# Second attention of a graph kernel: sums in the step of their scores, and three DVE operands kept in PSUM

## The reference, cut to what matters

```
xp = (x @ W).reshape(n, H, C)                        # H = 4 heads, C = 64
a_src = einsum('nhc,hc->nh', xp, att_src)
a_dst = einsum('nhc,hc->nh', xp, att_dst)
alpha = leaky_relu(a_src[src] + a_dst[dst], 0.2)
amax = segment_max(alpha, dst)
ex = exp(alpha - amax[dst])
denom = segment_sum(ex, dst)
agg = segment_sum(xp[src] * (ex / denom[dst])[..., None], dst)
out = elu(agg.reshape(n, H * C) + bias)
x = layernorm(x + out)
```

## Time and profile before

| what | value |
|---|---|
| median of 3 runs | 5005.02 us (5001.28 to 5005.71) |
| profiled execution, its own time | 5004.25 us |
| its span in the trace | 5002.2 us |
| mean granted TensorE clock | 0.739 of full speed |
| PE busy | 3443.0 us (69%) |
| POOL busy | 3316.7 us (66%) |
| DVE busy | 3196.3 us (64%) |

### The profile page before, as it was taken

How to read it: one execution, slowest core, us unless ns; L and a number is a source line. 1 busy time by engine, 2 the same in 40 slices (tenths; PEclk the granted TensorE clock), 3 DMA queues, 4 the chain that set the end, 5 groups by cost and what they waited for, 6 DMA issues and landing times.

```text
span 5002.2 us, 159594 instructions
## 1 busy us (share of the span) xinstructions
PE 3443.0 (69%) x54244; PEld 2420.8 (48%) x54244; DVE 3196.3 (64%) x9015; ACT 1477.6 (30%) x3981; POOL 3316.7 (66%) x3229
## 2 busy tenths in 40 slices
PE   7978988888888888888455455555545455555554
PEld 4645555555555555555344343444434343444433
DVE  3236888888888888888645555555555555555555
ACT  2325555555555555555200101101000100101011
POOL 1227777777777777777267767777776777676763
PEclk9989999999999999999755555555555555555555
DMA  6879999899999999998234444444444444444443
GB/s 211 282 219 266 266 271 266 265 266 264 266 266 266 266 264 266 267 266 266 83 103 125 120 119 120 117 123 116 122 122 119 118 121 121 118 122 116 124 115 82
DMA packets 690509, 924.71 MB, mean 185 GB/s; under 512 B 351175, under 2 KB 526880, under 8 KB 690208
## 3 DMA queue, kind: packets, MB, share of 16 engines
q0 software_dynamic: 200064, 627.60, 42.6%
q1 hardware_dynamic: 488830, 291.63, 21.8%
q10 hardware_dynamic: 1314, 0.99, 0.1%
HBM read 791.40 MB, written 127.61 MB: 184 GB/s over the span
## 4 chain that ended last, share of the span: by engine, by line
PE 25%; POOL 9%; DMA 9%; issue 5%; DVE 2%; POOLq 0%; ACT 0%; DVEq 0%; SPq 0%
POOL plain_rows L1386 9%; DMA plain_rows<-xp,plain_index 9%; PE plain_p_o L1512 8%; PE plain_p_o L1515 4%; PE plain_p_a L1477 4%; PE plain_p_a L1478 3%; PE plain_p_s L1491 2%; PE plain_p_o L1520 1%; PE plain_p_o L1524 1%; DVE plain_damped L1553 1%; DVE plain_score L1555 1%; PE plain_p_a L1480 1%; PE plain_p_a L1481 1%; PE plain_p_s L1492 0%; PE plain_p_a L1483 0%
## 5 line engine op out<-in xcount | busy, mean ns | idle before, releaser
L1386 POOL DMA_INDIRECT plain_rows<-xp,plain_index x1563 | 1748.5, 1119 | 807.6 <-issue 436.9
L840 POOL DMA_INDIRECT typed_rows<-kv,typed_index x1563 | 1495.8, 957 | 564.1 <-issue 442.2
L1477 PE MATMUL plain_p_a<-plain_a_dst,plain_home 128*128 128x16 f32 x786 | 230.1, 373 | 1089.0 <-DMA plain_rows<-xp,plain_index 1062.5
L1477 PEld LDWEIGHTS plain_p_a<-plain_a_dst,plain_home 128*128 128x128 f32 x786 | 208.9, 326 | 1099.5 <-issue 1099.4
L949 PE MATMUL typed_p_s<-typed_kt,typed_q 64*32 64x416 f32 x4168 | 471.8, 520 | 202.4 <-issue 160.4
L1241 ACT ACTIVATE typed_weight<-typed_weight,typed_col 128x416 f32<-128x416 f32 x521 | 334.8, 643 | 878.1 <-DVE typed_col L1073 849.9
L1044 DVE TENSOR_TENSOR typed_kt<-typed_p_kt,typed_rel 128x768 f32<-128x768 f32 x521 | 494.1, 948 | 5.2 <-PE typed_p_kt L926 5.1
L1071 DVE CUSTOM_DVE_ANT_0 typed_weight<-typed_p_s,typed_far 128x416 f32<-128x416 f32 x521 | 305.6, 587 | 296.6 <-PE typed_p_s L949 270.0
L1512 PE MATMUL plain_p_o<-plain_rows,plain_spread 128*32 128x65 f32 x12504 | 461.1, 315 | 3.8 <-DVE plain_spread L1594 3.8
L926 PE MATMUL typed_p_kt<-all_cst,typed_rows 128*128 128x128 f32 x3126 | 429.0, 274 | 11.2 <-DMA typed_rows<-kv,typed_index 10.5
L1553 DVE TENSOR_SCALAR plain_damped<-plain_p_a 128x64 f32<-128x64 f32 x131 | 29.5, 225 | 596.0 <-PE plain_p_a L1483 596.0
(11 more groups left out here) (224 smaller groups left out, 6610.5 us busy)
## 6 DMA issues: line engine op xcount, KB each, us to landing
typed_match<-match SPq DMA_DIRECT2D x131, 208.0 KB
agg<-qkv_zero SPq DMA_DIRECT2D x98, 264.0 KB, 2.5
typed_agg<-agg SPq DMA_DIRECT2D x98, 264.0 KB
plain_agg<-agg SPq DMA_DIRECT2D x98, 264.0 KB, 3.8
kv<-qkv_kv SPq DMA_DIRECT2D x98, 258.0 KB
typed_kinds<-match SPq DMA_DIRECT2D x131, 192.0 KB
typed_rows<-kv,typed_index POOLq DMA_INDIRECT x1563
plain_rows<-xp,plain_index POOLq DMA_INDIRECT x1563
```

Source lines behind the costliest of these rows:

```text
L840: pool.indirect_dma_start(rows[:, r, j, :], None, k.kv, bass.IndirectOffsetOnAxis(ap=index[:, g, at:at + 1], axis=0)).then_inc(rows_in[r], 16)
L1386: pool.indirect_dma_start(rows[:, r, i, j, :], None, k.xp, bass.IndirectOffsetOnAxis(ap=index[:, g, at:at + 1], axis=0)).then_inc(rest_in[ ...
L1477: pe.matmul(p_a[:, at:at + LANES], home[:, j * P:j * P + P], a_dst[:, m], start=True, stop=False, skip_group_check=True)
```

## The change

PE's list has `aggregate` behind `turn_tops`, with a lag of 1 in place of 2: in a step PE makes the scores of batch b, turns them, turns its maxima, and makes its sums. The lags of all other parts stay. Three operands of DVE move from SBUF into a PSUM tensor `p_x` that was used at the start of the stage only: `running` (written and read by the scans, bank 0), `weight` (written by ACT, read by L1594) and the row of node numbers, copied there once (read by L1578; both in bank 1).

```diff
-        running = z.sb("running", [P, SLOTS])
-        weight = z.sb("weight", [P, KEYS])
+        running, weight, line = p_x[:, 0, 0:SLOTS], p_x[:, 1, 0:KEYS], p_x[:, 1, KEYS:KEYS + TN]
...
-            by_batch(pe, PE_FIRST, PE_UNROLL, BatchPart(1, add_scores), BatchPart(1, turn_scores), BatchPart(2, aggregate), BatchPart(1, turn_tops))
+            by_batch(pe, PE_FIRST, PE_UNROLL, BatchPart(1, add_scores), BatchPart(1, turn_scores), BatchPart(1, turn_tops), BatchPart(1, aggregate))
...
                 v.tensor_tensor(one[:].rearrange("p (e i) n -> p e i n", i=TPB),
-                                cst[:, C_LINE:C_LINE + TN].unsqueeze(1).unsqueeze(1).broadcast_to((P, EDGES, TPB, TN)),
+                                line.unsqueeze(1).unsqueeze(1).broadcast_to((P, EDGES, TPB, TN)),
...
-                                weight[:].rearrange("p (e h) -> p e h", h=HEADS).unsqueeze(3).broadcast_to((P, EDGES * TPB, HEADS, TN)),
+                                weight.rearrange("p (e h) -> p e h", h=HEADS).unsqueeze(3).broadcast_to((P, EDGES * TPB, HEADS, TN)),
...
+            then(v.tensor_copy(line, cst[:, C_LINE:C_LINE + TN]))
             v.sem_inc(setup, 1)
...
-                act.activation(weight[:], gap[:], ACT.Exp).then_inc(exp_done, 1)
+                act.activation(weight, gap[:], ACT.Exp).then_inc(exp_done, 1)
```

## The result

The changed kernel takes 4854.79 us (median of 4 runs, 4849.29 to 4858.85) against 5005.36 before: a ratio of 0.970 (95% interval 0.9683 to 0.9717), 3.0% faster. The forecast was 4770 us. The result lies inside the stated range, at its very end, with 151 us gained in place of 235.

The account below looks back on a forecast made before the run. PE and POOL wait for each other in a ring. The new ring, 2231 us, after 2492.46 and before a 33.6 us tail makes 4757; 10 for late join and 2.05 around it lead to 4770 us, range 4735 to 4860.

Parts of the forecast that it names:

- The ring: New chain from scores through scans, spread and sums to next scores: 16.15 us a step, 17.36 with a block of nodes.
- The tail behind the last sums: Stores, loads and last blocks after the stage's last sums: 33.6 us, in both versions.
- the hand-over: From the end of the sums to the next scores on PE: 0 us, upper bound 0.2.
- the 8 us that it removed: PE's idle time each old step for three gathers and their landing, about 8 us, gone with the new order.
- join late: Slow a_dst DMAs sometimes delay join and the scans, by up to 1.8 us; 10 us added over 95 steps.
- PSUM costs nothing: DVE operations reading PSUM operands take no longer: 0 us taken, loss bound 0.5 us a step or 65 us.
- PSUM gains nothing in this order: POOL has slack in the new ring, so its calls freed by PSUM operands are worth 0.
- the old ring: Before the change: sums, three gathers with landing, scores, turn, sums; steps of 19.1 us with PE and POOL waiting for each other.
- (a): Rival: loads late in most block steps, a ring of 18.6 us of its own, 4875 us; chance 0.07.
- (c): Rival: broadcasting from PSUM at half rate slows L1594 and L1578, 2.66 us a step, 5118 us; chance 0.04.
- (b): Rival: PSUM operands don't free POOL, calls stay stretched, 17.8 us a batch, 4860 us; chance 0.07.
- (d): Rival: PE's granted clock rises from 5 tenths, 3 us a step go, 4390 us; chance 0.04.

Follow-up runs that it names:

- the run with the blocks moved: Changed kernel with PE's loop of 42 steps, join and weigh_parts moved behind spread_weights on DVE, scale behind weigh on ACT: 4655.96 us, ratio 0.9305.
- the last run: Kernel before with three operands in PSUM and 4 slots of rows, plus join moved between find_tops and mark_nodes on DVE: 4541.64 us, ratio 0.9087.

## Why the prediction came out as it did

- **The ring: right.** Sum 16.15 and 17.36 us, measured 16.15 and 17.48. Most of the 0.12 is in leak to first scan (2.47 for my 2.40) and in the sums (5.42 for 5.36). The tail behind the last sums was 33.6 us, and is 33.2.
- **The step that failed is the hand-over:** "The next scores follow at once, their rows, home and a_dst being there; I take 0 for the hand-over, and 0.2 as the upper bound." In 20 of 130 steps it is about 4.2 us, the turn of PE's loop: 20 x 4.16 = 83 us, nearly all of what was missed (4854.79 less 4770 is 85). The run with 42 steps a turn, 4777.97 us, lands 8 from the forecast. That it is so near is in part luck: block steps that are 0.12 us longer add 11 us, and the 10 us for a late join did not come. The turn was in the kernel before too, at the same place, and the profile of before could not show its price: it put PE's idle time down to the rows, which came later still. That is what the prediction should have asked of the 8 us that it removed: what else ends within them.
- **join late: wrong by its 10 us.** In 3000 to 4700 DVE waited for that DMA 1.3 us in all, five times. SP's chain was timed rightly: in the step shown above its last load goes at 3602.61, 8.9 us behind the end of the scan (8.8 in the prediction). The delays that were added on top hardly ever reached DVE.
- **PSUM costs nothing: right.** L1593 2288 ns for 2292, with broadcasts from PSUM. The access overhead that the Trainium skill states ("Perfetto Trace Analysis", section "Optimizing Scalar/DVE Operations"), larger in PSUM, doesn't show on these operations here: the scans are at 1017 ns (output in PSUM, 1008 before) and 1007 (input, 1012 before).
- **PSUM gains nothing in this order: right, and a half truth.** Calls went from 1126 to 954 ns in the mean, as the section "Who interferes with whom" of "SBUF — State Buffer" in the Trainium skill would have it, and the order alone gives the same time. But each part was priced only with the other in place. The prediction had the call of 2.97 us on the old ring in its own first paragraph. With 2.0 us less there, 131 x 2.0 = 262 us is what PSUM alone should bring (285 measured), more than the sum for both. The order then costs: 4726 becomes 4855.
- **Rivals.** (a) and (c) are out by these rows. (b) is out as a fact, calls being freed, and its steps of 17.8 us did not come even with the calls stretched: in the run of the order alone steps without a turn last 16.2 and 17.6 us. That its 4860 us lie near the measured time is chance. (d): the clock stayed at 5 tenths in every kernel here, also at four slots, where PE is busy for 6 tenths of the stage.

## What to carry to other kernels

When a wait leaves an engine's ring, whatever ended shortly before that wait is next; here it was the turn of a loop. The new order took a transfer out of PE's ring and put a chain of other engines in; a fourth buffer slot took it out without that price, so try the slot first. And price each part of a change alone: here the one that looked like cover for the other was worth nearly twice the whole, 285 us against 151.

## What the runs showed of the hardware

- The turn of PE's loop left PE idle for 3.7 to 4.7 us (4.1 in the mean; 4.3 us per turn by the difference of run times), with a body of 6 steps of about 185 matmuls each. With a body of 42 steps the pauses were 4.35 and 4.07 us, and 5.35 and 4.98 in the run with the blocks moved. The profile has no releaser for it, it says "issue".
- An indirect DMA call of POOL that begins under a DVE operation with two SBUF inputs stands until that ends, then needs 0.82 us more (0.75 to 0.78 behind the second scan of the kernel before). A call begun just before one was not held in front of L1594 (93 of 93 in the run of the order alone), but was in front of L1603 (78 of 78 in the last run), where a DVE operation of 0.40 us cost a call 0.65. One of L1594's inputs moved to PSUM, the call is back at 0.94 us beside an operation just as long.
- From the end of the sums to POOL's first call 0.87 to 0.94 us pass, in the kernel before, with PSUM alone and in the changed kernel, where DVE is idle meanwhile.
